# x scales of groups two to seven and all o quantisation on GpSimd, with new instruction orders on all engines

## What is computed

```python
def bitlinear(x, w):
    xn = rmsnorm(x)
    s = 127.0 / clip(max(abs(xn), -1), 1e-5)
    xq = clip(round(xn * s), -128, 127) / s
    ws = 1.0 / clip(mean(abs(w)), 1e-5)
    wq = clip(round(w * ws), -1, 1) / ws
    return einsum('bld,od->blo', xq, wq)

def attn(x):
    f = sigmoid(bitlinear(x, Wf))
    i = silu(bitlinear(x, Wi)) * (1 - f)
    h = scan over the tokens: h = f * h + i
    g = bitlinear(x, Wg)
    o = rmsnorm(g) * g_norm_weight * (h * sigmoid(h))
    return bitlinear(o, Wo)

x = layernorm(x + attn(x))
y = experts(x): silu(x @ ctx[e].T) * (x @ ctx[e].T) @ ctx[e].T   # the token's expert e
x = layernorm(x + y)
x = layernorm(x + einsum('btd,rde->bte', x, factors) / sqrt(8) + bias)
```

## Time and profile before

| | us |
|---|---|
| median of 3 runs | 343.01 (340.66 to 343.08) |
| the profiled execution | 342.06 |
| its span, first to last instruction | 340.3 |
| PE busy | 278.1 (82%) |
| DVE busy | 226.3 (66%) |
| ACT busy | 229.6 (67%) |
| POOL busy | 190.8 (56%) |

### The profile page before, as it was taken

How to read it: one execution, slowest core, us unless ns; L and a number is a source line. 1 busy time by engine, 2 the same in 40 slices (tenths; PEclk the granted TensorE clock), 3 DMA queues, 4 the chain that set the end, 5 groups by cost and what they waited for, 6 DMA issues and landing times.

```text
span 340.3 us, 5734 instructions
## 1 busy us (share of the span) xinstructions
PE 278.1 (82%) x1505; PEld 211.9 (62%) x1518; DVE 226.3 (66%) x488; ACT 229.6 (67%) x456; POOL 190.8 (56%) x381
## 2 busy tenths in 40 slices
PE   1376646484879899999999998998999999999760
PEld 1253414252557678787778876676888888887540
DVE  2789999999987879968677696454543434543310
ACT  4687789889678769986887686476555644554530
POOL 2536765858637748865565856547444444454442
PEclk9999989879799999999999999999999999999975
DMA  7999981987593782013003002205111111000000
GB/s 233 387 388 387 225 196 62 185 153 143 130 227 79 115 179 65 1 62 126 0 33 141 17 15 111 62 7 186 56 40 56 62 66 62 33 26 29 4 6 0
DMA packets 17406, 37.02 MB, mean 109 GB/s; under 512 B 1503, under 2 KB 1631, under 8 KB 17376
## 3 DMA queue, kind: packets, MB, share of 16 engines
q0 software_dynamic: 6496, 15.74, 19.6%
q1 hardware_dynamic: 10880, 20.92, 19.2%
HBM read 26.68 MB, written 10.76 MB: 110 GB/s over the span
## 4 chain that ended last, share of the span: by engine, by line
PE 62%; ACT 9%; issue 5%; DVE 5%; DMA 2%; POOL 2%; ACTq 0%; POOLq 0%; DVEq 0%; SPq 0%
PE bank_y L1455 5%; PE bank_z L1455 5%; PE bank_y L1456 5%; PE bank_z L1456 5%; PE bank_z L1459 5%; PE bank_y L1459 5%; PE bank_m L1455 4%; PE bank_m L1456 4%; PE bank_m L1459 4%; PE bank_tr L1424 3%; PE bank_c L1357 2%; PE bank_q L1424 2%; PE bank_a L1357 1%; PE bank_b L1357 1%; DMA sorted_rows<-r,place 1%
## 5 line engine op out<-in xcount | busy, mean ns | idle before, releaser
L312 POOL TENSOR_SCALAR n_v<-n_dev 128x1 f32<-128x1 f32 (+1 forms) x46 | 8.8, 192 | 52.2 <-ACT x L644 26.7
L1455 PE MATMUL bank_y<-c_hi,h_hi 128*128 x76 | 31.8, 418 | 1.8 <-ACT h_hi L612 1.4
L996 DVE TENSOR_TENSOR act_z<-bank_z,act_z 128x512 f32<-128x512 f32 x19 | 13.1, 689 | 30.1 <-ACT act_z L626 30.1
L1455 PE MATMUL bank_m<-f_hi,m_hi 128*128 128x512 f32 x76 | 32.1, 423 | 0.8 <-ACT m_hi L612 0.8
L353 POOL TENSOR_TENSOR x<-x,bias_b 128x512 f32<-128x512 f32 x19 | 24.6, 1293 | 14.5 <-PE bank_q L1424 14.5
L1455 PE MATMUL bank_z<-c_hi,a_hi 128*128 x76 | 30.4, 400 | 2.8 <-ACT a_hi L612 1.5
L1456 PE MATMUL bank_m<-f_lo,m_hi 128*128 128x512 f32 x76 | 30.8, 405 | 0.0
L1456 PE MATMUL bank_y<-c_lo,h_hi 128*128 x76 | 30.1, 396 | 0.0
L1456 PE MATMUL bank_z<-c_lo,a_hi 128*128 x76 | 30.1, 395 | 0.0
L612 ACT ACTIVATE h_hi<-bank_tr 128x512 fp32r<-128x512 f32 x19 | 11.3, 596 | 26.7 <-PE bank_tr L1424 26.7
L313 POOL TENSOR_TENSOR n_d<-n_v,minus_half 128x1 f32<-128x1 f32 (+1 forms) x46 | 27.1, 588 | 3.8
(11 more groups left out here) (205 smaller groups left out, 848.7 us busy)
## 6 DMA issues: line engine op xcount, KB each, us to landing
f_sum<-in_factors POOLq DMA_DIRECT2D x7, 1024.0 KB
rows<-sorted_rows SPq DMA_DIRECT2D x19, 256.5 KB, 2.9
xs<-in_x SPq DMA_DIRECT2D x8, 512.0 KB, 7.6
c_stage<-in_ctx_t SPq DMA_DIRECT2D x4, 1024.0 KB, 14.3
sorted_rows<-pad_row SPq DMA_DIRECT2D x1, 1539.0 KB, 18.3
w_stage<-in_wf_t SPq DMA_DIRECT2D x1, 1024.0 KB, 8.7
w_stage<-in_wi_t SPq DMA_DIRECT2D x1, 1024.0 KB, 10.8
w_stage<-in_wg_t SPq DMA_DIRECT2D x1, 1024.0 KB, 13.0
```

What stands on the lines that cost most here:

```text
L996: v.tensor_tensor(act_z[:], bank_z[:], act_z[:], ALU.mult).then_inc(s.hid, 1)
L1455: t.matmul(bank[:], hi[:, c, :], w_hi(c), start=(c == 0), stop=False)
```

## The change

- The four-instruction `scale_x` stays on DVE for groups 0 and 1. For groups 2 to 7 a new `scale_x_pool` computes the same on POOL in five instructions: product, maximum, power of -1, times 127, product.
- `quantise_o` of DVE is gone; POOL does all eight groups, so groups 0 to 2 are new there.
- The lists of PE, ACT, DVE and POOL and the bodies of the loop over the turns 5 to 7 are put in a new order, and the list for the end of group 7. SP's list and the last slots' loop stay.
- Of the moves, in the lists: `max_o(p, 1)` directly follows `max_o(p, 0)`; `scans(1, 1)` is ahead of `residual_1(0)`; `low_of_ctx` of chunks 0 and 1 go ahead of group 0's gates and others later; `add_factor(2)` is ahead of `scale_x_pool(3)`, `add_factor(3)` ahead of `quantise_o(1)`, `add_factor(4)` ahead of `power_1(1)` and `scale_o(2)`; `weight_sum(W_G)` is ahead of `weight_ready(W_F)`.

The diff, cut: the new function, POOL's list, ACT's list for groups 1 and 2, DVE's list for the same groups, and the turns of DVE and PE.

```diff
@@ -262,6 +262,18 @@
                     link(pool.tensor_scalar(x_ve[:], x_ss[:, i, :], 1.0 / D, EPS, ALU.mult, ALU.add), s.xch)
                     link(pool.tensor_tensor(x_r[:, i, :], x_ve[:], minus_half[:], ALU.pow), s.xch)
 
+                def scale_x_pool(g):
+                    i = g % 2
+                    pool.wait_ge(s.xch, XCH * (g + 1))
+                    pool.wait_ge(s.mxx, GT * g + GT)
+                    link(pool.tensor_tensor(x_mr[:], x_max[:, i, :], x_r[:, i, :], ALU.mult), s.xsc)
+                    after(pool, s.mcb, g - 1)
+                    pool.tensor_scalar(x_mc[:, i, :], x_mr[:], GUARD, None, ALU.max).then_inc(s.x_mc, 1)
+                    pool.wait_ge(s.x_mc, g + 1)
+                    link(pool.tensor_tensor(x_rc[:, i, :], x_mc[:, i, :], minus_one[:], ALU.pow), s.xsc)
+                    link(pool.tensor_scalar(x_mr[:], x_rc[:, i, :], QMAX, None, ALU.mult), s.xsc)
+                    pool.tensor_tensor(x_q[:, i, :], x_mr[:], x_r[:, i, :], ALU.mult).then_inc(s.xq_s, 1)
+
                 def scale_g(g):
                     i = g % 2
                     pool.wait_ge(s.xq_s, g + 1)
@@ -407,74 +419,84 @@
                 power_x(0)
                 power_x(1)
                 fill_events()
+                weight_ready(W_F)
                 number_slots()
-                weight_ready(W_F)
                 weight_ready(W_I)
                 open_slots()
                 weight_ready(W_G)
                 places()
+                scale_g(0)
                 add_factor(1)
-                scale_g(0)
                 power_x(2)
+                scale_x_pool(2)
                 scale_o(0)
+                quantise_o(0)
                 weight_ready(W_O)
+                power_x(3)
                 scale_g(1)
-                power_x(3)
+                add_factor(2)
+                scale_x_pool(3)
                 number_rows(0)
+                scale_o(1)
                 power_1(0)
-                add_factor(2)
+                add_factor(3)
+                quantise_o(1)
                 pool.wait_ge(s.padded, 16)
                 scatter_rows(0)
-                scale_o(1)
-                add_factor(3)
                 scale_g(2)
                 power_x(4)
+                scale_x_pool(4)
+                add_factor(4)
+                power_1(1)
                 number_rows(1)
-                power_1(1)
-                add_factor(4)
                 scale_o(2)
+                quantise_o(2)
                 scatter_rows(1)
                 scale_g(3)
+                add_factor(5)
                 power_x(5)
-                add_factor(5)
                 number_rows(2)
                 power_1(2)
                 scatter_rows(2)
-                token_of_row(0)
+                scale_x_pool(5)
                 scale_o(3)
                 quantise_o(3)
                 add_factor(6)
                 power_2(0)
-                token_of_row(1)
-                add_bias(0)
                 scale_g(4)
+                number_rows(3)
                 power_x(6)
-                number_rows(3)
                 add_factor(7)
                 power_1(3)
-                token_of_row(2)
+                token_of_row(0)
                 power_2(1)
                 scatter_rows(3)
+                scale_x_pool(6)
+                token_of_row(1)
+                token_of_row(2)
+                add_bias(0)
 
                 for turn in range(MERGE + 2, N_GROUPS):
                     g, p, n = turn, turn - 1, 2 * turn - LEAD
-                    number_rows(p)
+                    token_of_row(n)
                     scale_o(p)
                     quantise_o(p)
+                    scale_g(g)
...
@@ -661,123 +683,126 @@
                 weight_sum(W_I)
...
                 square_o(0, 1)
-                tanh_f(1, 0)
-                high_of_ctx(0, range(1, 4))
                 tanh_f(1, 1)
+                square_x(3, 0)
+                silu_i(1, 0)
+                square_x(3, 1)
+                high_of_ctx(1, range(0, 1))
+                x_by_channel(2)
+                max_row(2)
                 square_g(1, 0)
-                silu_i(1, 0)
-                forget(1, 0)
+                weight_ready(W_O)
+                o_by_channel(0)
+                silu_i(1, 1)
                 forget(1, 1)
-                x_by_channel(2)
-                high_of_ctx(1, range(0, 1))
-                weight_ready(W_O)
-                silu_i(1, 1)
-                o_by_channel(0)
+                high_of_ctx(1, range(1, 2))
+                silu_h(1, 0)
                 square_g(1, 1)
-                max_row(2)
-                silu_h(1, 0)
-                high_of_ctx(1, range(1, 3))
-                square_x(3, 0)
-                square_x(3, 1)
+                high_of_ctx(1, range(2, 3))
+                silu_h(1, 1)
+                square_o(1, 0)
+                square_o(1, 1)
+                tanh_f(2, 0)
                 square_1(0)
                 high_of_ctx(1, range(3, 4))
-                silu_h(1, 1)
                 square_x(4, 0)
+                silu_i(2, 0)
+                tanh_f(2, 1)
+                square_g(2, 0)
+                high_of_ctx(2, range(0, 1))
+                silu_i(2, 1)
                 norm_1(0)
-                square_o(1, 0)
-                square_g(2, 0)
-                square_o(1, 1)
-                square_g(2, 1)
-                tanh_f(2, 0)
-                high_of_ctx(2, range(0, 2))
-                tanh_f(2, 1)
                 x_by_channel(3)
-                silu_i(2, 0)
                 forget(2, 0)
-                silu_i(2, 1)
+                square_x(4, 1)
                 forget(2, 1)
                 o_by_channel(1)
+                max_row(3)
+                square_g(2, 1)
+                high_of_ctx(2, range(1, 2))
+                silu_h(2, 0)
                 high_of_ctx(2, range(2, 3))
-                max_row(3)
-                square_x(4, 1)
+                silu_h(2, 1)
...
@@ -894,13 +919,6 @@
                     dve.wait_ge(s.x_rc, g + 1)
                     v.scalar_tensor_tensor(x_q[:, i, :], x_rc[:, i, :], QMAX, x_r[:, i, :], ALU.mult, ALU.mult).then_inc(s.xq_s, 1)
 
-                def quantise_o(p):
-                    dve.wait_ge(s.oq_s, p + 1)
-                    dve.wait_ge(s.sqo, GT * p + GT)
-                    for j in range(GT):
-                        tile = o_tok[:, p % 2, j, :]
-                        v.tensor_scalar(tile, tile, o_q[:, j:j + 1], HALF_MAGIC, ALU.mult, ALU.add).then_inc(s.qo, 1)
-
                 def quantise_x(g):
                     dve.wait_ge(s.xq_s, g + 1)
                     after(dve, s.tx, g)
@@ -1085,145 +1103,135 @@
                     v.tensor_scalar(slot_off[:], bank_m[:, 0:N_SLOTS], float(KC), None, ALU.mult).then_inc(s.slot_off, 1)
...
                 output(0, 0)
-                rescale_f(1, 0)
                 output(0, 1)
                 max_o(0, 0)
+                max_o(0, 1)
                 rescale_i(1, 0)
+                quantise_x(2)
                 rescale_i(1, 1)
-                rescale_f(1, 1)
-                max_o(0, 1)
-                scale_x(2)
-                quantise_x(2)
+                gate_i(1, 0)
                 round_weights(W_O)
-                quantise_o(0)
-                gate_i(1, 0)
+                low_of_ctx([2])
+                scans(1, 0)
+                slot_offsets()
+                low_of_ctx([3])
+                max_x(3, 1)
+                gate_i(1, 1)
                 weigh_g(1, 0)
-                max_x(3, 1)
-                slot_offsets()
-                low_of_ctx([0])
-                scans(1, 0)
-                gate_i(1, 1)
-                low_of_ctx([1])
+                scans(1, 1)
+                residual_1(0)
                 weigh_g(1, 1)
-                residual_1(0)
-                scans(1, 1)
-                rescale_f(2, 0)
-                scale_x(3)
-                low_of_ctx([2])
-                rescale_f(2, 1)
                 output(1, 0)
                 output(1, 1)
-                low_of_ctx([3])
+                rescale_f(2, 0)
                 max_o(1, 0)
+                max_o(1, 1)
+                low_of_ctx([4])
+                rescale_f(2, 1)
                 rescale_i(2, 0)
-                low_of_ctx(range(4, 6))
+                quantise_x(3)
+                rescale_i(2, 1)
                 max_x(4, 0)
-                max_o(1, 1)
-                quantise_x(3)
+                gate_i(2, 0)
                 weigh_g(2, 0)
-                rescale_i(2, 1)
-                low_of_ctx([6])
+                gate_i(2, 1)
                 max_x(4, 1)
-                quantise_o(1)
-                low_of_ctx([7])
-                gate_i(2, 0)
-                gate_i(2, 1)
...
@@ -1232,36 +1240,35 @@
                     rescale_f(g, 0)
                     rescale_f(g, 1)
                     hidden(n - 1)
+                    max_o(p, 0)
```

(38 more changed lines are left out.)

291 lines of the change are left out of this document (147 added, 144 removed).

## The result

The changed kernel takes 353.39 us (median of 4 runs, 351.73 to 354.71) against 342.41 us for the kernel before beside it. The ratio is 1.0359 with an interval of 1.0312 to 1.0407: 3.6% slower. The forecast was 340.5 us and its range ended at 344.5.

The account below looks back on a forecast made before the run. DVE was taken to bound 27 to 99 us, PE's passes later. Terms 1.4 + 1.0 + 0 + 0 - 0.3 = 2.1, taken as 2.5 with overlap: 343.0 - 2.5 = 340.5 us, range 336.8 to 344.5.

Parts of the forecast that it names:

- What bounds the kernel: 27 to 99 us bound by DVE, busy 70.59 of 72; later PE's passes; gain is PE's full stretch beginning sooner.
- project_back(0) at 49.2 to 49.5, gain 0: Group 0 in the head: quantise_o(0) on POOL ends about 47.5, project_back(0) stays near the old 49.39.
- project_back(1) at 68.3, ACT last: Group 1 in the head: ACT, not DVE, sets project_back(1), at 68.3 against 69.64, gain 1.3 us.
- rival 3: POOL's queue: add_factor(3) ahead of quantise_o(1), add_factor(4) ahead of scale_o(2) delay both; about 3.5 us slower, 346.5; chance 0.14.
- The port: DVE and POOL colliding: 3 collisions of 0.24, 0.7 us on DVE, which has that air; 0 in the sum.
- rival 2: Each of six moved instructions stops DVE for its whole length, at most 5.4 us: 341.9, no change; chance 0.11.
- project_back(2) and the first product: Group 2 and first slots: project_back(2) at 86.1 against 87.20, gain 1.1; first expert product 95.8 against 97.19.
- up(0) 1.4 sooner: First slots: project_i(4) and up(0) come 1.4 us sooner, 97.19 to 95.8, a term of the sum.
- The holes from 99 to 121 (+1.0): Of PE's 1.86 us idle between 99 and 121, the new order fills about 1.0.
- The turns (0 to -0.3 each): Turns 5 to 7: no gain, a loss of 0 to 0.3 us a turn; the sum takes one, -0.3.
- The end (0): End of group 7: keeps its chain of residual, norm, scatter and load; 0 of PE's 3.36 us idle counted.
- Rival 4: Gain up to 99 us is lost in 99 to 121, slots waiting for scattered rows: 342.5 to 343; chance 0.09.

Follow-up runs that it names:

- a_two_early: Changed kernel with group 0's scatter chain put forward on ACT and POOL and max_row(1) directly behind silu_i(0, 1): 358.1 us, ratio 1.0501.
- a_quant_dve: Changed kernel with quantise_o of groups 0 to 2 back on DVE at the old list's places: 353.06 us, ratio 1.0324.
- b_turns: Kernel before with both moves to POOL and old lists, plus only the new bodies of turns 5 to 7: 347.46 us, ratio 1.0164.
- b_both_pool: Kernel before with quantise_o of groups 0 to 2 and scale_x of groups 2 to 7 on POOL, old orders: 345.11 us, ratio 1.0122.
- b_tail: Kernel before with both moves to POOL, old lists and turns, plus only the new end of group 7: 345.33 us, ratio 1.01.

## Why the prediction was wrong

- **What bounds the kernel.** Right that DVE was full from 27 to 99 us and that the head and its joint with the full stretch would decide: 10.0 of the 11.6 us lie there. Wrong in the step from there: "bound by DVE" was read as a stock of work that gets smaller, and the chain through scatter_rows, which DVE itself waits for (6.4 us) and on which the load of slot 0's rows hangs, was not walked. It was in the source, one line of residual_1 and one of load_rows, and the kernel before shows no wait at either, because its order kept the scatters early.
- **project_back(0) at 49.2 to 49.5, gain 0.** It came at 51.19. In the profiled execution the loads came 1.56 us sooner than before, so the list lost 3.4 us here. 1.0 of it lies ahead of project_f(0): ACT does weight_sum(W_G) ahead of weight_ready(W_F), which I listed as a move and gave no price. From W_F's first instruction to project_f(0) it takes 8.31 to 8.47 us in all nine kernels with the old list and 9.35 to 9.48 in the eleven with the new one. ACT's timeline before and after, from that instruction to project_f(0)'s weights:

```profile
10.85 1.91 ACT L523 ACTIVATE w_q<-w_stage 128x2048 bf16<-128x2048 f32 x1 [1.94 <-DMA w_stage<-in_wf_t]
...
17.85 1.06 ACT L528 ACTIVATE w_q<-w_stage 128x1024 bf16<-128x1024 f32 x1 [0.77 <-DVE w_stage L1039]
```

```profile
9.29 1.91 ACT L545 ACTIVATE w_q<-w_stage 128x2048 bf16<-128x2048 f32 x1 [0.52 <-DMA w_stage<-in_wf_t]
...
15.46 1.90 ACT L545 ACTIVATE w_q<-w_stage 128x2048 bf16<-128x2048 f32 x1
17.26 0.19 ACT L545 ACTIVATION_READ_ACCUMULATOR w_q<-w_stage 128x1 f32 x1
17.35 2.17 ACT L550 ACTIVATE w_q<-w_stage 128x1024 bf16<-128x1024 f32 x2
```

  The other 2.3 has two candidates that lie beside each other. project_f(1) is late by max_row(1), a move that was not in my walk, which began at quantise_o(0). And transpose_o(0) waits 3.73 us for POOL's quantise_o(0), which began at 46.20 and not 44.3 and took 3.12 us. With max_row(1) early again project_back(0) is no sooner (33.3 in a_two_early), and with quantise_o back on DVE neither (32.5 in a_quant_dve); either seems to be enough.
- **project_back(1) at 68.3, ACT last.** It came at 71.82. Counted from project_back(0) it took 20.6 us, before 20.3, and I had 19. Not ACT but POOL was last: transpose_o waited 2.85 us for quantise_o(1), a pair of 3.24 us that began at 66.80 and that I had at 63.1 with 1.6. That is rival 3's place: add_factor(3) waited 1.18 us for add_factor(2)'s transfer, over the 1 us that I had set as the sign. The walk's 0.6 us of air was gone with add_factor(2), issued at 54.65 and not 52.2, whose transfer then took 11.0 us and not 9.3.
- **The port.** The term of 0 was mis-sized: 2.3 us on DVE and about 1.2 us a pair on POOL, against 0.7 and nothing. The low parts' mean of 763 ns passed the 0.75 us that I had named for rival 2. The rule of the Trainium skill ("SBUF — State Buffer", "Who interferes with whom"), that the two lock each other out, points the right way: both sides lost. Its upper bound in rival 2, 5.4 us on DVE, was further off than my 0.7; the trace shows longer instructions, not the lock itself. The one collision of 0.24 us that I took from the earlier trace rows was a mild case, and what it did to POOL I did not ask.
- **project_back(2) and the first product.** 91.69 and 106.68 for 86.1 and 95.8. This is the step that failed: the walk took the spacings of the old trace with scatter_rows(0), and what waits for it, at nothing. Up to project_back(2) DVE's missed wait of 4.27 us for the late scatter of group 0 stands in the chain; alone, in the kernel before, such lateness makes a wait of 5.87 us and costs 6 us of the median, here it lies beside POOL's delay. From there to the first product I had 9.7 us and it took 15.0, with the slow load of slot 0's rows, 6.3 us. The "up(0) 1.4 sooner" of the sum became 9.5 later.
- **The holes from 99 to 121 (+1.0).** PE was busy 17.00 of 22 us, before 20.14; its full stretch had not begun.
- **The turns (0 to -0.3 each).** -0.4 each up to turn 7, and about -2.3 us of the median by b_turns over b_both_pool. Sign right, size short.
- **The end (0).** Right for the new order of that list (b_tail). That PE had no slack there against the landing of group 7's scatter, where a wait of 2 us brings a slow clock with it, I had not seen.
- **Rivals.** None of them gives 353. Rival 3 was the nearest in place, on POOL's queue between add_factor and quantise_o, but it followed quantise_o to project_back and not the scatter behind it in the same list. Rival 4 named the slots that wait for rows, but only as a place where the gain is lost. POOL's 61 us are set against 69 us in one place of the prediction and against 66 in another; the stage has 72, and POOL was busy 56.69 of them.

What the runs leave open: the changed kernel has 10 us more in the head and no fall of the clock at the end, while seven others with the new turns, some with a better head and some not, take 164.6 to 167.9 us from turn 7 to the end, 3 to 6 more. Why the rows come late in those and not in it was not found. Nor was a kernel made in which only the load of slot 0's rows is moved out of the way of add_factor(5). So the 3.6% are located, but no experiment gave them back.

## What to carry to other kernels

When a piece is moved or an order is changed, list for each buffer that is used again (here r1) who must have let go of it, and give each such release its new time; a wait that the old trace shows as zero is the one to fear, since the old order is why it is zero. Do the same for each small load on the path that comes to stand behind a large transfer: half of the loss up to turn 5 goes with one load of 257 KB that took 6.3 us and not 2.8. Of the fullest engine, relief and a stall look the same in a table of shares, and only the count of finished instructions tells them apart. And move work to POOL only by its price beside DVE's two-input instructions, here 2.1 to 3.8 us a pair and not the 1.8 of a late turn.

## What was not expected of the hardware

- A pair of 128x512 tensor_scalar on POOL took 1.80 us in a late turn and 3.12, 3.24 and 1.94 in the head of the changed kernel. Small ones suffer too: a 128x2 o_a took 1.32 us and o_q 1.74, against 0.20 to 0.40 elsewhere.

```profile
44.79 1.32 POOL L300 TENSOR_SCALAR o_a<-o_mc,w_mean 128x2 f32<-128x2 f32 x1
...
85.32 1.74 POOL L296 TENSOR_TENSOR o_q<-o_rc,o_r 128x2 f32<-128x2 f32 x1
```

- The granted clock fell from 1.00 in the stretch from 240 to 245 us to 0.52 in the next, behind waits of 2.00 and 0.78 us on PE, and made 2.0 us into 4.7.
- From the last scatter to the load that waits for it, it took 3.4 to 4.0 us in fifteen of the twenty executions and 5.0 in five, with nothing between. Group 0's scatters, beside a transfer of 1 MB, took 5.6 and 6.3 us from issue to landing in the changed kernel and 8.4 and 9.8 in a_quant_dve.
- The load of slot 0's rows took 2.6 to 2.9 us in fourteen executions and 5.6 to 6.3 in the five in which it started 1.2 to 1.4 us after the issue of a 1 MB transfer.
